# TensorE's loop over the batch: a body of eight elements in place of two

## The reference, cut to what matters

```python
x = x + conv1d(x, W0, padding=4, groups=4) + (cond @ cw0.T)[:, :, None] + side[None, :, None]
for l in (1, 2):
    h = gelu(gelu(cond @ w0[l] + b0[l]) @ w1[l] + b1[l])
    att = softmax(h @ w2[l] + b2[l])                       # (128, 8)
    agg_w = einsum('bk,koi->boi', att, weight[l])          # one 128x128 matrix a batch element
    x = x + einsum('boi,bih->boh', agg_w, x) + (att @ bias_k[l])[:, :, None]
x = x + conv1d(x, W3, padding=4, groups=4) + (cond @ cw3.T)[:, :, None] + side[None, :, None]
```

## Time and profile before

| what | value |
|---|---|
| median of 3 runs | 3321.71 us (3309.91 to 3323.68) |
| profiled execution, its own time | 3333.55 us |
| its span, first to last instruction | 3331.8 us |
| TensorE busy | 92% of the span |
| VectorE, ScalarE busy | 34%, 21% |
| mean granted TensorE clock | 0.981 |
| DMA moved | 368.15 MB, mean 110 GB/s |

### The profile page before, as it was taken

One profiled execution on the slowest core, in us unless ns is written; L12 is line 12 of the kernel. 1 busy time (PEld: TensorE's weight loads), 2 busy tenths in 40 slices (PEclk: granted clock), 3 DMA queues, 4 the chain that ended last, 5 costly groups with the idle time before them and its releaser, 6 DMA issues.

```text
span 3331.8 us, 173286 instructions
## 1 busy us (share of the span) xinstructions
PE 3072.0 (92%) x80196; PEld 1869.3 (56%) x80196; DVE 1141.9 (34%) x3099; ACT 688.0 (21%) x784; POOL 1.0 (0%) x13
## 2 busy tenths in 40 slices
PE   7999999999999999999999989989999999899998
PEld 4555555555565565555555555556555555565555
DVE  4333333333333343333333333334333333333332
ACT  2212212121222121221212222212121212121222
POOL 0000000000000000000000000000000000000000
PEclk9999999999999999999999999999999999999999
DMA  4444444444444444444444444444444444444443
GB/s 124 109 115 110 113 106 119 106 116 104 110 115 111 108 115 110 108 110 106 119 106 116 105 111 113 112 107 117 109 114 107 106 119 113 106 108 116 108 113 82
DMA packets 188753, 368.15 MB, mean 110 GB/s; under 512 B 20683, under 2 KB 105683, under 8 KB 171603
## 3 DMA queue, kind: packets, MB, share of 16 engines
q1 hardware_dynamic: 185744, 354.11, 41.5%
q10 hardware_dynamic: 2242, 1.53, 0.2%
HBM read 204.56 MB, written 150.99 MB: 107 GB/s over the span
## 4 chain that ended last, share of the span: by engine, by line
PE 92%; issue 7%; DMA 0%; DVE 0%; ACT 0%; SPq 0%; ACTq 0%
PE banks L454 78%; PE banks L471 12%; PE banks L462 2%; DMA small<-in_small 0%; PE banks L537 0%; DMA m_rows<-m_saved 0%; DMA m_saved<-m_pair 0%; DVE x_lo L355 0%; PE banks L549 0%; PE banks L519 0%; DVE vec_part L412 0%; ACT L275 0%; DVE bias L416 0%; PE banks L507 0%; SPq L178 0%
## 5 line engine op out<-in xcount | busy, mean ns | idle before, releaser
L454 PE MATMUL banks<-x_in,taps 32*32 32x512 f32 x36864 | 1372.5, 619 | 191.0 <-issue 187.4
L454 PE MATMUL banks<-x,taps 32*32 32x512 f32 x36864 | 1375.9, 596 | 42.7 <-issue 42.4
L454 PEld LDWEIGHTS banks<-x,taps 32*32 32x32 f32 x36864 | 887.2, 103 | 419.3 <-issue 143.2
L454 PEld LDWEIGHTS banks<-x_in,taps 32*32 32x32 f32 x36864 | 648.6, 104 | 751.4 <-issue 552.2
L240 ACT CAST x_hi<-banks 128x1024 fp32r<-128x1024 f32 x256 | 246.7, 1016 | 1303.2 <-PE banks L454 1303.2
L374 DVE SCALAR_TENSOR_TENSOR mixed<-expert,mix,mixed 128x128 f32<-128x128 f32 x1792 | 481.6, 345 | 0.2 <-issue 0.2
L363 DVE TENSOR_TENSOR x<-banks,bias_now 128x1024 f32<-128x1024 f32 x128 | 156.7, 1224 | 881.4 <-PE banks L454 881.4
L381 DVE COPY m_t<-banks 128x128 f32<-128x128 f32 x128 | 37.3, 291 | 1057.2 <-PE banks L462 1057.2
L247 ACT ACTIVATE x<-banks,bias_now 128x512 f32<-128x512 f32 x256 | 162.3, 686 | 1062.5 <-PE banks L454 1062.5
L471 PE MATMUL banks<-x_hi,m_rows 32*128 32x512 f32 x4096 | 364.2, 406 | 8.8 <-DMA m_rows<-m_saved 8.8
L355 DVE TENSOR_TENSOR x_lo<-banks,x_hi 128x1024 fp32r<-128x1024 f32 x256 | 301.4, 1219 | 188.2 <-ACT x_hi L240 188.2
(11 more groups left out here) (59 smaller groups left out, 50.9 us busy)
## 6 DMA issues: line engine op xcount, KB each, us to landing
x_in<-in_x SPq DMA_DIRECT2D x128, 1024.0 KB, 7.2
out<-x SPq DMA_DIRECT2D x512, 256.0 KB, 3.7
m_rows<-m_saved SPq DMA_DIRECT2D x512, 128.0 KB, 5.6
m_saved<-m_pair SPq DMA_DIRECT2D x128, 128.0 KB, 1.7
taps<-in_W SPq DMA_DIRECT2D x8, 144.0 KB, 9.9
expert<-in_e ACTq DMA_DIRECT2D x2, 512.0 KB, 14.5
expert_t<-in_e_t SPq DMA_DIRECT2D x1, 512.0 KB, 10.1
small<-in_small ACTq DMA_DIRECT2D x1, 458.5 KB, 6.8
```

The costliest lines, as they stand in the source:

```text
L454: mm = nc.tensor.matmul(tile[rows_of(p), g, :], taps[l][rows_of(g), t, g, :], row[rows_of(g), N * p + t:N * p + t + N], start=(t == 0), st ...
```

## The change

TensorE's loop body holds eight elements instead of two: elements 2 to 7 are written out ahead of the loop, which goes over elements 8 to 119 in 14 passes, and elements 120 to 127 are written out behind it. The order of the work, the waits and the other engines' loops stay as they are.

```diff
+        SPAN = 4
+
...
             for b in range(1, ODD):
                 step(b, b % ODD, b // ODD)
-            with pe.Fori(1, B // ODD - 1) as i:
-                for odd in range(ODD):
-                    step(ODD * i + odd, odd, i)
-            for b in range(B - ODD, B):
+            for b in range(ODD, ODD * SPAN):
+                step(b, b % ODD, b // ODD)
+            with pe.Fori(1, B // (ODD * SPAN) - 1) as i:
+                for n in range(ODD * SPAN):
+                    step(ODD * SPAN * i + n, n % ODD, SPAN * i + n // ODD)
+            for b in range(B - ODD * SPAN, B):
                 step(b, b % ODD, b // ODD, last=(b == B - 1))
```

## The result

The changed kernel takes 3224.6 us in the median of 4 runs (3218.2 to 3230.9), against 3322.7 us for the kernel before: ratio 0.969, interval 0.966 to 0.972. It is faster by 3.1%, where 5.6% was forecast, and lies 35 us above the range. Direction and mechanism held; two prices and the step from the profiled execution to the median did not.

The account below looks back on a forecast made before the run. TensorE was taken as the bound, its 7% of issue as waits for code. 3333.6 - 222 + 24 + 10 = 3146 us for the profiled execution, 11.9 us less for the median, said as 3135 us; range 3085 to 3190.

Parts of the forecast that it names:

- (a): TensorE's loop end: 48 jumps fewer, each costing 4.63 us with the hole and slow restart behind it, -222 us.
- (b): Behind a jump: next piece of code comes after some 20 matmuls instead of 76, 1.85 us more per jump, +24 us.
- (d): Other engines: they keep their loops and still keep up with the shorter time per element, no cost.
- hidden: Rival: fetching pieces of straight code costs TensorE nothing, 3044 us; chance 0.06.
- the wait moves: Rival: without holes TensorE stands at waits on x3, x4 or the spread matrix, about 3320 us; chance 0.04.
- slower: Rival: pieces of code come late at every start in straight code, 3863 us; chance 0.02.
- starves in every element: Rival: straight code loses 1.30 us in each of 126 elements, 164 us instead of 91, 3208 us; chance 0.06.
- (c): Holes in straight code, at conv 4: 0.72 us an element, 91 us over 126 elements, +10 us against before.
- (e): TensorE's clock dip beside a jump: lies inside the hole's time, counted as nothing; up to 21 us could be added.

Follow-up runs that it names:

- unroll: The changed kernel with TensorE's elements 1 to 127 all written out, no loop and no jump: 3127.4 us, ratio 0.942 to the kernel before.
- tiny_x: The changed kernel with each load of x from element 2 on bringing only 16 of 2,048 columns: one execution, a span of 3084.8 us.

## Why the prediction was right and where it was wrong

**Right.** (a) The cause of the 7% of "issue": pieces of code. The branch keeps 3.93 us in the median, and the 48 jumps less took 122.5 us off the "end" column (159.2 to 36.7; 2.6 and 2.8 us a jump). (b) The place: 19 records against 20, the next piece at 4.11 us against 4.41; the issue before conv 1's matmuls came out at 70.2 us, as worked out. Packets of code: 664 against 655. The clean element stayed 22.8 us, and no wait on x3, x4 or the spread matrix came behind the first element, in any kernel (d). The rivals "hidden", "the wait moves" and "slower" are excluded by the 83.6 us of holes, by the list of waits and by the result; "starves in every element" (3208 us) is nearest to the time, also in its own term (164 us, where 134.6 were measured and I had 91), and wrong in its detail: some elements of the eight have no hole and some lose 2.6 us.

**Wrong: step (c), mis-sized.** I took 0.72 us an element and it is 134.6 / 126 = 1.07: 44 us more than the 91 counted. The bound of 1.30 came from one hole at one place. By place in an element, in the mean over the passes of the changed kernel, what the eight elements of the body lose is 1.02, 1.97, 0.85, 0.82, 0.86, 0.00, 0.17 and 2.64 us; the last, with its hole after 473 matmul records of the element, shows that five records behind the hole of the old body (after 468, 1.26 us) the loss doubles. `unroll` shows the same at these places (1.25 and 3.12 us), so it is the place and not the jump that follows. I had taken 1.30 us as the most that an element could lose, and let it fall from there with the place in the burst; the highest is over twice that. By the Trainium skill, "Runtime: NRT & Kernel Launch", section "Instruction fetch mechanics", the end of a block is crossed mostly hidden: `tiny_x` agrees (2.3 us of issue), and every kernel with the full load in one burst doesn't.

**Wrong: step (e), counted as nothing.** The dip had cost next to nothing before because the second hole covered it: 27 of the 61 jumps had one, and the first taps took 6.52 us with it and 6.37 without. With the hole moved to 19 matmul records after the jump, all 13 jumps have a dip. It begins around the start of the hole, lasts 6.8 us for most jumps and outlasts the hole by 4.1 us in the mean: a jump costs 113.4 / 13 = 8.7 us, where (a) and (b) make 6.5. That is 29 us; 1.8 to 2 us of each jump are the slow taps seen in the chain. The 13 jumps show that these are the clock's: where the dip outlasts the hole by 2.8 us the taps behind it take 5.5 us, and where by 5.9 us they take 6.9; a straight line through all 13 gives 4.3 us and 0.43 us more for each us of the dip. I had named 21 us as possible and left them out of the sum.

**Wrong: the step to the median.** The sum stood at 3146 us for the profiled execution, and I took 11.9 us off, because the profiled execution before was above its median. The one after was the fastest of four, 6.4 us below. Together 18 us, and this part is chance: which execution was profiled. The miss in the median, 3224.6 - 3135 = 90, is so 44 + 29 + 18 = 91. The range had counted half of (c)'s rest and most of (e), but not that both would come with the median's 12 us besides.

**Open.** Why a hole at one place costs twice that of its neighbour (1.97 us in the second element of the body, 0.85 in the third; in `unroll` 1.98 after 544 records, 0.95 after 548) isn't settled; nor why taps at full clock behind a rest take 5.2 us instead of 4.39 when no hole is seen in them. Whether the second half of the load helps by being short or by being late is open too.

## What to carry to other kernels

"Issue" idle on an engine with a long body, at fixed places where the code waits for nothing, was here code that wasn't there yet: look at the branch's duration, at the queue of instructions and at what the DMA engines do in that moment. Fewer jumps help, but first see where the target stands in its piece, and whether large transfers start just when a piece is asked for; halving a burst and moving it gave about as much as the longer body (104 us over the clean element against 117), and more where both places of a body lay in the burst (189 us in the padded body of two). And when a stall is moved, price anew what it used to cover: here the clock's dip came out of the hole that had hidden it.

## What the runs showed of the hardware that I had not expected

Twelve small matmuls ahead of the loop changed the time by 1.8% (ratios 0.969 and 0.951), forty by 2.3% the other way in the body of two (14 of 69 us are the forty themselves). A queue of stores delays a fetch of code by 1.1 us in the mean (4.03 to 2.95 us), and the load of x with the spreads costs an element up to 2.6 us at one place of the changed kernel (3.1 in `unroll`), in the mean.

A hole ends 1.2 to 1.9 us after the last byte of the piece of code that it waited for. And the price of a jump is that of its target's code: TensorE's branch kept 3.95 us in the median, while those of VectorE, ScalarE and SyncE, with 61 to 63 records each in the same trace and far shorter bodies, took at most 67 ns.
